# Swapping two VectorE instructions, the layer norm's last and the first layer's closing add, in a four-layer residual kernel

## The reference: what is computed

```
x = x + x @ W0[subject].T + b0[subject]                # 8 subjects, 512 x 512
x = x + rotate pairs of rows by angles from delta_t    # a 128 x 128 mix
x = x + x @ W[category] + b[category]                  # 64 categories, 512 x 512
x = x + layernorm(x + relu(x @ W1[lang] + b1) @ W2[lang] + b2) * gamma + beta
```

## Time and profile before

| what | value |
|---|---|
| time, median of 3 runs | 1185.45 us (1184.38 to 1187.25) |
| profiled execution | 1187.25 us, its span 1185.4 us |
| TensorE matmul busy | 1104.8 us, 93% of the span |
| VectorE busy | 966.5 us, 82% |
| ScalarE busy | 790.7 us, 67% |
| GpSimd busy | 730.4 us, 62% |
| mean granted TensorE clock | 0.986 of full |

### The profile page before, as it was taken

One profiled execution on the slowest core, in us unless ns is written; L12 is line 12 of the kernel. 1 busy time (PEld: TensorE's weight loads), 2 busy tenths in 40 slices (PEclk: granted clock), 3 DMA queues, 4 the chain that ended last, 5 costly groups with the idle time before them and its releaser, 6 DMA issues.

```text
span 1185.4 us, 29185 instructions
## 1 busy us (share of the span) xinstructions
PE 1104.8 (93%) x6042; PEld 926.3 (78%) x6042; DVE 966.5 (82%) x1382; ACT 790.7 (67%) x1829; POOL 730.4 (62%) x801
## 2 busy tenths in 40 slices
PE   1779999999599999999999899999999999999996
PEld 1568888888478888888788788887788887787884
DVE  5758888888488888888888888888888888888886
ACT  2546767677466767677767667777676767677674
POOL 5446666666366666666666666665666666666664
PEclk9989999999899999999999999999999999999998
DMA  6597777775497777777779677778777778687761
GB/s 212 196 368 240 256 247 255 246 257 198 160 300 246 234 265 256 246 257 248 254 245 299 230 255 243 257 249 274 238 256 244 254 251 289 195 311 233 259 221 62
DMA packets 97564, 290.67 MB, mean 245 GB/s; under 512 B 11870, under 2 KB 12510, under 8 KB 79676
## 3 DMA queue, kind: packets, MB, share of 16 engines
q1 hardware_dynamic: 95736, 287.98, 72.7%
q10 hardware_dynamic: 1604, 0.42, 0.2%
HBM read 254.53 MB, written 33.84 MB: 243 GB/s over the span
## 4 chain that ended last, share of the span: by engine, by line
PE 84%; DVE 4%; issue 4%; DMA 2%; ACT 2%; ACTq 1%; DVEq 1%; SPq 1%; POOL 1%; POOLq 1%
PE ps_mix L1061 10%; PE ps_l L1050 9%; PE ps_l L1085 9%; PE ps_l L1034 9%; PE ps_l L1079 9%; PE ps_l L1075 9%; PE ps_hT L1105 9%; PE ps_l L1045 5%; PE ps_x3T L1095 4%; PE ps_l L1038 4%; PE ps_y L1118 3%; PE ps_y L1116 2%; PE ps_y L1115 2%; DMA gamma_sb<-gamma 1%; DVE w_lo L874 1%
## 5 line engine op out<-in xcount | busy, mean ns | idle before, releaser
L874 DVE TENSOR_TENSOR w_lo<-w_in,w_hi 128x1024 fp32r<-128x1024 f32 x256 | 397.4, 1552 | 0.8 <-issue 0.8
L470 POOL TENSOR_TENSOR w_in<-w_in,ident 128x512 f32<-128x512 f32 x128 | 165.9, 1296 | 271.4 <-DVE w_lo L874 255.2
L608 ACT ACTIVATE w_hi<-w_in 128x1024 fp32r<-128x1024 f32 x256 | 257.2, 1052 | 82.7 <-PE ps_l L1079 69.0
L653 ACT ACTIVATE x3T<-ps_x3T,minus_bup 128x128 f32<-128x128 f32 x512 | 146.0, 367 | 72.1 <-PE ps_x3T L1095 71.0
L507 POOL TENSOR_TENSOR x<-x,beta_sb 128x512 f32<-128x512 f32 x128 | 166.2, 1298 | 38.8 <-issue 29.4
L477 POOL TENSOR_TENSOR x_lo<-x_in,x_hi 128x512 fp32r<-128x512 f32 x127 | 163.7, 1289 | 11.9 <-ACT x_hi L582 11.9
L884 DVE TENSOR_TENSOR x<-ps_l,b_sb 128x512 f32<-128x512 f32 x128 | 88.4, 691 | 93.9 <-PE ps_l L1050 93.9
L1034 PE MATMUL ps_l<-w_hi,x_hi 128*128 128x512 f32 x512 | 151.3, 418 | 0.0
L1061 PEld LDWEIGHTS ps_mix<-mix,x 128*128 128x128 f32 x1024 | 126.9, 194 | 28.9 <-issue 28.0
L1105 PE MATMUL ps_hT<-x3T,w_in 128*128 128x128 f32 x1024 | 137.8, 278 | 11.5 <-DMA w_in<-W 11.5
L1085 PE MATMUL ps_l<-w_lo,x2T_hi 128*128 128x512 f32 x512 | 138.8, 391 | 7.9 <-DVE w_lo L874 7.9
(11 more groups left out here) (145 smaller groups left out, 1910.2 us busy)
## 6 DMA issues: line engine op xcount, KB each, us to landing
w_in<-W SPq DMA_DIRECT2D x128, 1024.0 KB, 5.0
x_in<-xT SPq DMA_DIRECT2D x128, 256.0 KB, 3.9
w_in<-W SPq DMA_DIRECT2D x128, 256.0 KB, 2.8
out<-yb SPq DMA_DIRECT2D x128, 256.0 KB, 3.0
b_in<-bias_rows SPq DMA_DIRECT2D x126, 256.0 KB, 4.4
w_in<-W0T SPq DMA_DIRECT2D x7, 1024.0 KB, 5.2
wup_sb<-Wup SPq DMA_DIRECT2D x1, 2560.0 KB, 9.4
beta_sb<-beta_rows SPq DMA_DIRECT2D x1, 2560.0 KB, 9.1
```

The costliest lines, as they stand in the source:

```text
L470: pool.tensor_tensor(diagonal_of(w2_in[s % WB]), diagonal_of(w2_in[s % WB]), ident[:, :].unsqueeze(1).broadcast_to([P, C, P]), ALU.add).th ...
L608: act.activation(w2_hi[:, halves[n]], w2_in[s % WB][:, halves[n]], ACT.Copy).then_inc(w2_hi_made, 1)
L874: dve.tensor_tensor(w2_lo[:, half], w2_in[s % WB][:, half], w2_hi[:, half].bitcast(fp32), ALU.subtract).then_inc(w2_lo_made, 1)
```

## The change

In VectorE's queue `finish_norm(s-2)` (L933, with the waits it had) is put ahead of `finish_l0(s+1)` (L884), in each step from s = 2 on; at s = 127 there is no `finish_l0` and the order stays. Nothing is added or removed, and the queues of TensorE, ScalarE, GpSimd and SyncE are the same word for word.

```diff
--- before.py
+++ after.py
@@ -984,9 +984,9 @@
                     centre(s - 2)
                 if s >= 2:
                     finish_l2(s)
+                    finish_norm(s - 2)
                     if s < LAST:
                         finish_l0(s + 1)
-                    finish_norm(s - 2)
                 add_x3(s - 1)
             centre(LAST - 1)
             finish_norm(LAST - 1)
```

## The result

The changed kernel takes 1193.59 us (median of 6 runs, 1190.92 to 1196.16), the kernel before 1185.38 in the runs beside it (6 runs, 1183.86 to 1187.25): 8.2 us more. The ratio of the two is 1.0072, 95% interval 1.0054 to 1.0090. The forecast was 1192.5.

The account below looks back on a forecast made before the run. TensorE's own matmuls bound the regular step, with no slack behind L884. Terms 0 + 2.7 + 4.4 = +7.1 us gave 1194.35 on the profiled execution, 1192.5 against the median; range 1185.5 to 1202, likeliest case 1188 to 1197.

Parts of the forecast that it names:

- Regular steps, 0: Steps without a new W0 or late L507: length unchanged, L884 ready with 0.10 us to spare; 0 us.
- L1050 named as L884's releaser: Sign in the new profile: L884 still starts 1.44 after L901, with TensorE's L1050 as what releases it.
- the refund: L914, no longer behind L933, starts 0.20 us earlier, and the chain passes all of it to L507.
- the first reading: All else as it was: L884 0.10 us late in each of some 112 regular steps, 11 us.
- L507 late, +2.7: Steps where GpSimd's register read before L507 is late now delay L884: +2.7 us, between 0 and 5.
- Steps with a new W0, +4.4: Seven W0 loads, where late squares delay L507 and so L933 and L884: +4.4 us, between 0 and 8.6.
- The pair: A new-W0 step and the step after it: 0.36 + 0.41 = 0.77 us lost per W0.
- most of one: Of two neighbouring W0 round the 11.5 wait for W1, that wait swallows most of one W0's loss.
- The step forecast as harmless: New-W0 step: TensorE 0.82 us late at L1061, going under in its later 1.22 wait for the second L874.
- Rival C: L884 starts sooner behind its matmul, so L1061's weights load in time: -6.5 us, 1179 us; chance 0.08.
- Rival B: Delays of new-W0 steps and late L507 go under in waits and slack: 0 to 2 us; chance 0.19.
- Rival A: Chain gives nothing back, L933 bounds every regular step: +18, 1203.5 us, half of it 1198; chance 0.17.

Follow-up runs that it names:

- e4: Changed kernel with a copy of L933's work added behind L884, so that L914 starts as late as before the change: 1207.69 us.
- e1: Changed kernel, but with the old order in the 13 steps round a new W0: 1188.63 us against 1185.20 for the kernel before.
- e7: Changed kernel with idle identity matmuls filling TensorE's waits in six new-W0 steps, four ahead of the transposes and two ahead of `rotate`: 1192.76 us.
- e2: Kernel before the change, with the exchange only in the 13 steps round a new W0: 1190.21 us.
- e12: Changed kernel run once more, unaltered, for a second profile: 1195.24 us, ratio to the kernel before 1.0061 to 1.0089.
- e13: The kernel of e7 again, with idle matmuls in TensorE's waits, on the same chip as e12: 1193.35 us.
- e10: Changed kernel with three 128x1 instructions added on GpSimd between L488 and L507, making L507 later: 1205.32 us.

## Why the prediction was right

*Regular steps, 0.* Right, and for the reason given. The one sign that did not show is L1050 named as L884's releaser: L884 now waits too briefly for the view to list it, and its start at 1.43 has to stand for it. L914 came 0.21 earlier (0.20 foreseen), L507 0.20 earlier, L884 not later, with 0.08 to spare instead of 0.10. e4 takes the refund away and gets the 0.11 of the first reading.

*L507 late, +2.7.* Measured by e1 at 3.4 and in the profiles at 3.6 less 0.8. That the loss is 0.2 for a read of 0.5 is seen: steps 32, 73 and 119 are 0.23 to 0.24 longer. The large reads weigh more than I gave them: in the profile after one took 1.14 (s = 114) and cost 0.86.

*Steps with a new W0, +4.4.* The pair was put at 0.77 and measures 0.67 to 0.73 in three places where the clock stays up (59 and 60: 0.33 + 0.37; 108 and 109; 115 and 116), and 1.05 in 68 and 69. The five pairs together are 3.9 in e7's trace. The first two W0, next to each other, cost nothing against the trace of before, which has the lower clock in step 30, and 1.3 to 2.2 against those that don't (28 to 30: 44.6 to 44.9 in e2, e7, e12 and e13). The prediction's 5.4 less 4.4 takes off 1.0 where "most of one" of 0.77 can be no more than 0.77, so this part of the sum came near in part by luck. The term as a whole is 5.0 by e2 and 5.8 in the profile. What was not in it is the clock: the five pairs are 5.8 in the profile after, with two falls, and 3.9 in e7's without. The step forecast as harmless, TensorE's 0.8 going under in a later wait, is harmless only at the full clock.

*What hides what.* VectorE's queue behaved as assumed: in the trace after, L884 comes behind L933 in every step with the exchange, late L933 or not. Rival C did not come: L884 starts 1.43 after L901 in both orders. Rival B is excluded by e2. Rival A, priced at 1203.5, needs the refund to be missing; e4 takes it away and measures 1207.69.

The sum was 7.1 and the measured difference 8.2 (9.8 in e12). The 1.1 between the first two is about what the W0 steps (5.0 for 4.4) and the late reads (3.4 for 2.7) have more. The prediction also said that it would be wrong if the difference stood anywhere but at L1061; the lower clock behind the new waits is such a place, and it had not been thought of.

## What to carry to other kernels

A hole in a queue ahead of an instruction that the bounding engine waits for is not free to fill: what is put there must be ready in every step, late ones too, since its lateness is now everybody's. The regular step can come out even and single steps carry the whole loss, so read the slack of the regular step and then go through the steps that are not regular. When an instruction moves, follow also the one that moves up in its stead, and ask which engine the chain behind it hangs on: one that hangs on the bounding engine ahead of the delay takes part of a delay back (e10, 0.09 a step for 0.14), one that hangs on the delayed instruction none (e4).

## What the runs showed of the hardware that was not expected

TensorE's granted clock can fall to its lower level behind short waits, none longer than 1.6 us: in step 68 of the changed kernel behind waits of 1.50 and 0.50 us, for 6.8 us, and in step 87 behind 0.93, 0.20 and 0.61, for 3.4 us. Behind like waits in steps 59, 108 and 115 of the same trace it did not fall. By the step lengths such a fall cost 0.7 to 1.0 us in the two profiles of the changed kernel, and only some steps and runs have it. From step 59 on it came with the new order only (10 of 30 such steps, none of 25 in the old); in step 30 the kernel before had one too, behind a wait of 1.85.

A register read on GpSimd takes 0.20 in most steps. It takes 0.4 to 0.6 in 17 of the 128 of the changed kernel's trace (10 before) and 0.8 to 1.2 in two or three. One instruction of 0.19 us put ahead of the read makes L507 only 0.04 later, three make it 0.22 later.
